# Keys and queries of an attention layer: turned by TensorE, or by VectorE in 32x32 blocks and a trip through memory

## The chip, the cores and the metric

The kernel runs on one core of a Trainium2 chip. The metric is the device time of one execution in microseconds (us). The core has five engines that each work through a queue of their own in order: TensorE (PE, matrix products), VectorE (DVE), ScalarE (ACT), GpSimd (POOL) and SyncE (SP, which here only issues transfers). An engine stops at an instruction whose semaphore has not been reached, and everything behind it on that engine stops too. Transfers are issued from SP and from ACT.

## What is computed

Two transformer layers on 1024 tokens of width 512: a linear attention (L0), a mixture of low-rank experts, a softmax attention (L1) and a gated MLP, each added to its input and normalised. The change lies in the third, L1, with 32 heads of 128:

```
q = rmsnorm((x @ Wq + bq).reshape(1024, 32, 128), gq)      # per head, over its 128 values
k = rmsnorm((x @ Wk + bk).reshape(1024, 32, 128), gk)
v = (x @ Wv + bv).reshape(1024, 32, 128)
p = softmax(q @ k.T / sqrt(128))                           # per head, 1024 x 1024
y = (p @ v) per head @ Wo + bo                             # summed over heads
```

Each product is made in three passes, high times high, high times low and low times high: an operand is split into a rounded part (`_hi`) and what is left (`_lo`).

## The kernel before

The tokens are eight tiles (t = 0 to 7) of 128; two tiles make a batch (i = 0 to 3). The program of L1 is written out by hand for each engine as one `step` per head, which has eight slots (s = 0 to 7); a loop (`Fori`) runs two steps per turn, and the steps at both ends are written out. In step h, the slots score head h against its keys, tile by tile, while the values and outputs of head h and of head h-1 before it follow some slots later, and while the next heads are projected. An even slot and the odd slot behind it are called a pair here; a step has four pairs.

What PE does in a slot, in this order: half a batch of values (in an even slot; in an odd slot this comes last), one tile of projection (`project_tile`: 12 matmuls of 384 columns into `b_pj_kq`), one tile of scores (6 matmuls of 512 columns into `b_s_ps`), in odd slots four transposes (`transpose_kq`, below), one tile of output (3 matmuls of 512 columns into `b_y_ps`).

The way of a batch of keys and queries, before: DVE takes the projected tile out of `b_pj_kq` with its bias into `b_nat` (`take`); ACT squares it (`square`), DVE sums (`means`), POOL takes the inverse root (`inverse_rms`), ACT scales (`scale_kq`); PE turns keys and queries of both tiles, 128x128 each, into the other half of `b_pj_kq` (`transpose_kq`, line 1718); ACT copies that to `b_k_hi` and, times a gain, to `b_q_hi` (`kq_high`), DVE subtracts for `b_k_lo` and `b_q_lo` (`kq_low`). The scores of the next head wait for the last batch of this.

The way of a probability tile, before and after: DVE takes the row maximum (`maxima`) from `b_s_ps`, ACT the exponential (`exponent`), DVE turns the tile in 32x32 blocks (`transpose_blocks`, one STREAM_TRANSPOSE), ACT issues a write of the blocks to a scratch tensor in memory (`write_blocks`, 512 KB), SP reads them back in four transfers of 128 KB that put the blocks into their place (`move`), ACT rounds (`prob_hi`), POOL subtracts (`prob_lo`), PE multiplies with the values. SP works through these moves in order; each waits for its write.

Two PSUM limits tie DVE to PE: there is one bank for projections, so `project_tile` waits until the tile before has been taken; and two for scores, so the scores of tile t wait for the exponential of tile t-2.

Of the kernel before, what the change touches and what calls it, by code (L numbers as in the profile page):

```python
# [36 lines left out]
P = 128  # L37
# [1307 lines left out]
def l1_attention(nc, sh, ln_in, ln, aw, mlp, w, ow, bias, bo, gains):  # L1345
# [16 lines left out]
    with ExitStack() as ctx:  # L1362
# [6 lines left out]
        def sem(name):  # L1369
# [16 lines left out]
        nat = [sb(f"nat{i}", [P, BATCH, KQV]) for i in range(NB)]  # L1386
# [26 lines left out]
        pj_kq = bank("pj_kq", [P, TOK])  # L1413
        pj, kq_ps = pj_kq[:, 0:HALF], pj_kq[:, HALF:].rearrange("p (k n) -> p k n", k=2)
# [22 lines left out]
        const_in, bias_added, gain_ready = sem("const_in"), sem("bias_added"), sem("gain_ready")  # L1437
# [5 lines left out]
        def y_bank(h, t):  # L1443

            return pj if peeled(h, HEADS - 1) and t >= 3 and t % 2 else y_ps[:, :]
# [52 lines left out]
        def v_batch(h, b, cur, nxt, s):  # L1498

            if s % 2 == 0:  # L1500
                return None
            if s < 5:
                return (h, b, NB - 2 + s // 2) if cur else None
            return (h + 1, 1 - b, (s - 5) // 2) if nxt else None

        SPLITS = {1: 0, 2: 1, 4: 2}
# [5 lines left out]
        def by_tile(tile):  # L1512

            return tile[:, :].rearrange("p (u g q) -> p g u q", g=GROUPS, u=BATCH)

# [3 lines left out]
        def _(sp):  # L1519
# [42 lines left out]
        def _(pool):  # L1562
            def inverse_rms(g, bg, i):

                pool.wait_ge(mean_ready, NB * g + i + 1)
                wait(pool, exp_done, NT * (g - 1))
# [4 lines left out]
            def v_low(g, bg, i):  # L1571
                pool.wait_ge(v_hi_done, NB * g + i + 1)
                wait(pool, pv, NB * (g - 1))
                pool.tensor_tensor(v_lo[bg][:, BATCH * i:BATCH * (i + 1), :], nat[i][:, :, 2 * HD:],
                                   f(v_hi[bg][:, BATCH * i:BATCH * (i + 1), :]), ALU.subtract).then_inc(v_lo_done, 1)

# [7 lines left out]
            def step(h, b, cur, rest, nxt, more):  # L1584
                for s in range(NT):
                    if nxt and s % 2 == 0:
                        inverse_rms(h + 1, 1 - b, s // 2)
                    if v_batch(h, b, cur, nxt, s):
                        v_low(*v_batch(h, b, cur, nxt, s))
                    if split_batch(h, cur, rest, s):  # L1590
                        for part in range(2):
                            prob_lo(*split_batch(h, cur, rest, s), part)
# [13 lines left out]
        def _(act):  # L1606
# [3 lines left out]
            def square(g, i):  # L1610
                act.wait_ge(taken, NT * g + BATCH * (i + 1))
                wait(act, summed, NB * g + i)
                act.activation(sq[:, :, :, :].rearrange("p t k d -> p t (k d)"), nat[i][:, :, 0:2 * HD],  # L1613
                               ACT.Square).then_inc(squared, 1)

            def kq_high(g, bg, i):
                cut = slice(i * WIDE, (i + 1) * WIDE)
                act.wait_ge(kq_tr, NB * g + i + 1)
                wait(act, scored, NT * (g - 1))
                act.activation(k_hi[bg][:, cut], kq_ps[:, 0, :], ACT.Copy)  # L1620
                act.activation(q_hi[bg][:, cut], kq_ps[:, 1, :], ACT.Copy, scale=gain[:, 0:1]).then_inc(kq_hi_done, 1)  # L1621

            def v_high(g, bg, i):
                act.wait_ge(taken, NT * g + BATCH * (i + 1))
                wait(act, pv, NB * (g - 1))
                act.activation(v_hi[bg][:, BATCH * i:BATCH * (i + 1), :], nat[i][:, :, 2 * HD:],
# [7 lines left out]
            def scale_kq(g, bg, i):  # L1634

                act.wait_ge(rstd_ready, NB * g + i + 1)
                for u in range(BATCH):
                    for k in range(2):
                        part = nat[i][:, u, k * HD:(k + 1) * HD]
# [23 lines left out]
            def step(h, b, cur, rest, nxt, more):  # L1663
                if peeled(h, -1):
                    act.wait_ge(gain_ready, 1)
                for s in range(NT):
                    if nxt and s % 2 == 0:
                        square(h + 1, s // 2)
                    if v_batch(h, b, cur, nxt, s):
                        v_high(*v_batch(h, b, cur, nxt, s))  # L1670
# [6 lines left out]
                    if nxt and s % 2 == 0:  # L1677
                        scale_kq(h + 1, 1 - b, s // 2)
# [6 lines left out]
                    if cur:  # L1685
                        exponent(h, b, s)
                    if cur and s == 3:
# [9 lines left out]
        def _(pe):  # L1697
# [49 lines left out]
            def output_tile(h, b, t):  # L1747
# [4 lines left out]
                wait(pe, y_added, NT * h + (t - 1 if peeled(h, HEADS - 1) and t >= 3 else t))  # L1752
# [3 lines left out]
            def step(h, b, cur, rest, nxt, more):  # L1756
                for s in range(NT):
# [6 lines left out]
                    if nxt and s % 2:  # L1764
# [457 lines left out]
```

## Time and profile before

| | |
|---|---|
| median of 3 runs | 3012.76 us (3007.79 to 3013.55) |
| the profiled execution, its own time | 3011.74 us |
| its span, first to last instruction | 3009.8 us |
| its mean granted TensorE clock | 0.990 |
| PE busy over the span | 96% |
| DVE, ACT, POOL busy over the span | 74%, 53%, 65% |
| L1 attention, roughly | 1150 to 2745 us of the span |

Busy time is an average over stages that have different limits, so the stage that the change touches is read by itself in the rows below. In the view of stretches, the columns after each engine's name are its busy us and, in brackets, its instructions; the last three are the granted clock, the mean busy share of the 16 DMA engines and the GB/s that they moved. In a timeline a row is the start, the duration, the engine, the line, the instruction and its tiles; what stands in brackets at the end is the engine's idle time before it and what ended it. Matmuls overlap, so PE's pace is read from the difference between two starts, not from a duration.

### The profile page before, as it was taken

The numbers are of one execution on the slowest core, as the hardware profiler recorded it, in microseconds if no ns is written. First come the engines' busy times: TensorE is split into PE (matmuls) and PEld (weight loads), VectorE is DVE, ScalarE is ACT, GpSimd is POOL, SyncE is SP. The second block draws the span as 40 slices with busy tenths as digits, with TensorE's granted clock in tenths as the row PEclk, the third lists the DMA queues.
The fourth block names the chain that finished last, engine by engine and source line by source line (L and its number), as shares of the span: only waits on it lengthen the run. The fifth ranks groups of instructions, "written<-read, shape, count | busy, mean of one in ns | idle before, by whom it ended". The sixth has DMA issues, their size and how long they took to land. (4 is left out here: it accounts for less than half of the span.)

```text
span 3009.8 us, 55475 instructions
## 1 busy us (share of the span) xinstructions
PE 2886.3 (96%) x15712; PEld 2506.9 (83%) x15712; DVE 2236.4 (74%) x3420; ACT 1590.8 (53%) x3145; POOL 1952.6 (65%) x1525
## 2 busy tenths in 40 slices
PE   7999999999999977999999999999999999986998
PEld 5888888888888857898899899989898989975886
DVE  6787887887887856777777777777777777775555
ACT  4444444444444423666666666666666666652221
POOL 7777777777777632666666666666656666655664
PEclk9999999999999999999999999999999999998999
DMA  4334334334334401665666656666666656555551
GB/s 123 116 107 122 101 106 122 101 106 122 101 106 122 123 25 51 198 209 193 204 203 200 204 194 202 196 204 204 196 203 197 204 191 207 194 193 181 151 144 41
DMA packets 310073, 464.10 MB, mean 154 GB/s; under 512 B 30464, under 2 KB 220928, under 8 KB 305792
## 3 DMA queue, kind: packets, MB, share of 16 engines
q1 hardware_dynamic: 272336, 328.37, 37.8%
q10 hardware_dynamic: 37680, 135.02, 11.3%
q8 instruction: 29, 0.48, 0.1%
q14 instruction: 28, 0.23, 0.0%
HBM read 293.41 MB, written 169.87 MB: 154 GB/s over the span
## 5 line engine op out<-in xcount | busy, mean ns | idle before, releaser
L1660 ACT ACTIVATE b_prob<-b_s_ps,b_shift 128x1024 f32<-128x1024 f32 x256 | 286.1, 1118 | 347.2 <-DVE b_shift L1810 339.5
L82 PE MATMUL b_pj_kq<-b_w_hi,xT_hi 128*128 128x384 f32 x1008 | 351.8, 349 | 26.4 <-DVE b_nat L1786 24.5
L83 PE MATMUL b_pj_kq<-b_w_lo,xT_hi 128*128 128x384 f32 x1008 | 343.0, 340 | 0.0
L84 PE MATMUL b_pj_kq<-b_w_hi,xT_lo 128*128 128x384 f32 x1008 | 342.7, 340 | 0.0
L1816 DVE STREAM_TRANSPOSE b_blocks<-b_prob 128x1024 f32<-128x1024 f32 x256 | 317.3, 1239 | 28.4 <-ACT b_prob L1660 27.8
L1567 POOL TENSOR_TENSOR b_rstd<-b_mean_sq,power 128x4 f32<-128x4 f32 x128 | 129.0, 1008 | 320.7 <-DVE b_mean_sq L1796 314.1
L1582 POOL TENSOR_TENSOR b_pT_lo<-b_pT_lo,b_pT_hi 128x1024 fp32r<-128x1024 f32 x128 | 305.0, 2405 | 19.4 <-ACT b_pT_hi L1649 19.4
L1582 POOL TENSOR_TENSOR pT_lo<-pT_lo,pT_hi 128x1024 fp32r<-128x1024 f32 x128 | 305.0, 2406 | 13.9 <-ACT pT_hi L1649 13.9
L1810 DVE TENSOR_REDUCE b_shift<-b_s_ps 128x1 f32<-128x1024 f32 x256 | 306.8, 1199 | 2.7 <-PE b_s_ps L84 2.7
L82 PEld LDWEIGHTS b_pj_kq<-b_w_hi,xT_hi 128*128 128x128 f32 x1008 | 190.4, 189 | 63.4 <-DVE b_nat L1786 48.1
L1341 POOL TENSOR_TENSOR b_w_lo<-b_w_raw,b_w_hi 128x512 fp32r<-128x512 f32 x96 | 124.1, 1294 | 152.0 <-ACT b_w_hi L1334 134.5
L1793 DVE TENSOR_REDUCE b_sq_sum<-b_sq 128x4 f32<-128x512 f32 x128 | 87.8, 686 | 174.2 <-ACT b_sq L1613 174.2
L82 PE MATMUL b_s_ps<-b_k_hi,b_q_hi 128*128 128x512 f32 x512 | 201.0, 393 | 7.4 <-ACT b_prob L1660 7.4
L502 POOL TENSOR_TENSOR e_lo<-e_store,e_lo 128x256 fp32r<-128x256 f32 (+1 forms) x96 | 102.6, 1082 | 160.5 <-ACT e_lo L597 160.5
L84 PE MATMUL b_s_ps<-b_k_hi,b_q_lo 128*128 128x512 f32 x512 | 202.4, 395 | 0.0
L83 PE MATMUL b_s_ps<-b_k_lo,b_q_hi 128*128 128x512 f32 x512 | 201.5, 394 | 0.0
L83 PEld LDWEIGHTS b_pj_kq<-b_w_lo,xT_hi 128*128 128x128 f32 x1008 | 190.8, 189 | 0.6
L84 PEld LDWEIGHTS b_pj_kq<-b_w_hi,xT_lo 128*128 128x128 f32 x1008 | 190.6, 189 | 0.0
L990 DVE TENSOR_TENSOR a_acc<-a_acc,a_y_ps 128x512 f32<-128x512 f32 x243 | 164.8, 678 | 31.0 <-PE a_y_ps L84 31.0
L1837 DVE SCALAR_TENSOR_TENSOR x_nat<-b_y_ps,b_row_inv,x_nat 128x512 f32<-128x512 f32 x253 | 186.1, 736 | 2.3 <-PE b_y_ps L84 2.1
L1802 DVE TENSOR_TENSOR b_k_lo<-b_pj_kq,b_k_hi 128x256 fp32r<-128x256 f32 x128 | 54.3, 424 | 158.5 <-ACT b_q_hi L1621 158.4
L1640 ACT ACTIVATE b_nat<-b_nat,b_rstd 128x128 f32<-128x128 f32 x512 | 163.1, 391 | 13.1 <-POOL b_rstd L1567 13.1
(345 smaller groups left out, 9382.6 us busy)
## 6 DMA issues: line engine op xcount, KB each, us to landing
bounce<-b_blocks ACTq DMA_DIRECT2D x256, 512.0 KB, 3.5
pT_lo<-bounce SPq DMA_DIRECT2D x512, 128.0 KB, 3.1
b_pT_lo<-bounce SPq DMA_DIRECT2D x512, 128.0 KB, 2.8
kv_bounce<-a_kv_blocks SPq DMA_DIRECT2D x128, 256.0 KB, 3.8
a_kv_raw<-kv_bounce SPq DMA_DIRECT2D x32, 1024.0 KB, 4.8
b_w_raw<-in_w SPq DMA_DIRECT2D x32, 768.0 KB, 5.1
b_w_raw<-in_w SPq DMA_DIRECT2D x95, 256.0 KB, 3.2
a_w_raw<-in_w SPq DMA_DIRECT2D x32, 256.0 KB, 3.1
```

The costliest lines, as they stand in the source:

```text
L82: pe.matmul(out, w_hi, x_hi, start=first, stop=False, skip_group_check=partial)
L83: pe.matmul(out, w_hi, x_lo, start=False, stop=False, skip_group_check=partial)
L84: return pe.matmul(out, w_lo, x_hi, start=False, stop=last, skip_group_check=partial)
L990: dve.tensor_tensor(acc[:, t, :], acc[:, t, :], y_bank(h, t)[:, :], ALU.add).then_inc(y_added, 1)
L1341: pool.tensor_tensor(self.lo[b][:, :, cut], self.raw[:, :, cut], f(self.hi[b][:, :, cut]), ALU.subtract).then_inc(self.lo_done, 1)
L1567: pool.tensor_tensor(rstd[bg][:, BATCH * i:BATCH * (i + 1), :].rearrange("p t k -> p (t k)"), mean_sq[:, :, :].rearrange("p t k -> p (t k) ...
L1582: pool.tensor_tensor(lo, f(lo), f(hi), ALU.subtract).then_inc(pT_lo_done, 1)
L1640: last = act.activation(part, part, ACT.Copy, scale=rstd[bg][:, BATCH * i + u, k:k + 1])
L1660: act.activation(prob[t % 2][:, :], s_ps[t % 2][:, :], ACT.Exp, bias=shift[:, t:t + 1], accum_out=row_sum[:, t:t + 1]).then_inc(exp_done, 1)
L1810: dve.tensor_reduce(shift[:, t:t + 1], s_ps[t % 2][:, :], AX_X, ALU.max, negate=True).then_inc(shift_done, 1)
L1816: dve.transpose(blocks[t % 2][:, :, :, :].rearrange("p a m q -> p m a q"), prob[t % 2][:, :].rearrange("p (m a q) -> p m a q", a=GROUPS, q ...
L1837: dve.scalar_tensor_tensor(out=sh.x_nat[:, t, :], in0=y_bank(h, t), scalar=row_inv[:, t:t + 1], in1=sh.x_nat[:, t, :], op0=ALU.mult, op1=A ...
```

## The change

The transposes on PE go. A batch of keys and queries now takes the way of the probabilities:

- DVE turns the scaled keys and queries of a batch in 32x32 blocks (`turn_kq`, two STREAM_TRANSPOSE of 128x256), in the even slot of the pair after the one that scaled them;
- ACT issues a write of 256 KB to a scratch tensor (`write_kq`), SP reads it back in four transfers of 64 KB, in runs of 512 bytes (`move_kq`), into `b_kq_raw`;
- ACT multiplies the queries there by the gain, in place, and copies keys and queries to their high parts (`kq_high`: three instructions instead of two);
- POOL makes the low parts (`kq_low`: two subtractions of 128x256), which DVE made before.

Projections run two slots earlier, the weights of a head are split one or two slots earlier, and `square`, `means`, `inverse_rms` and `scale_kq` run a pair earlier. The half PSUM tile that held the turned keys and queries becomes a second bank for the outputs. In DVE's slot the probability blocks come first and `means` and `take` after; on ACT `scale_kq` moves behind the exponential; on POOL `inverse_rms` moves between the two halves of `prob_lo`. SP's step begins at tile 4 of the head before.

```diff
+        def projected(h, b, nxt, more, s):
-            if s < 6:
-                return (h + 1, 1 - b, s + 2) if nxt else None
-            return (h + 2, b, s - 6) if more else None
+            if s < 4:
+                return (h + 1, 1 - b, s + 4) if nxt else None
+            return (h + 2, b, s - 4) if more else None
+        def prepared(h, b, nxt, more, s):
+            i = s // 2 + 1
+            if i < NB:
+                return (h + 1, 1 - b, i) if nxt else None
+            return (h + 2, b, 0) if more else None
+        def turned(h, b, nxt, s):
+            return (h + 1, 1 - b, s // 2) if nxt and s % 2 == 0 else None
-        SPLITS = {1: 0, 2: 1, 4: 2}
+        SPLITS = {0: 0, 1: 1, 2: 2}
...
+            def move_kq(g, i):
+                sp.wait_ge(kq_written, 16 * (NB * g + i + 1))
+                sp.sem_inc(room, 1)
+                wait(sp, kq_lo_done, NB * g + i - 1)
+                for c in range(GROUPS):
+                    sp.dma_start(kq_raw[i % 2][c * BLK:(c + 1) * BLK].rearrange("y r k u x -> y r (k u x)"),
+                                 kq_bounce[i % 2][:, :, c, :].rearrange("r y n -> y r n")).then_inc(kq_moved, 16)
...
+                for t in range(NT // 2, NT):
+                    if t == 5 and cur:
+                        move_kq(h, 3)
+                    if t == 7 and nxt:
+                        move_kq(h + 1, 0)
+                    if rest:
+                        move(h - 1, t)
+                for t in range(NT // 2):
+                    if t % 2 and nxt:
+                        move_kq(h + 1, t // 2 + 1)
                     if cur:
                         move(h, t)
...
+            def kq_low(g, bg, i):
+                cut = slice(i * WIDE, (i + 1) * WIDE)
+                pool.wait_ge(kq_hi_done, 2 * (NB * g + i + 1))
+                pool.tensor_tensor(in_blocks(k_lo[bg][:, cut]), from_blocks(i, 0), f(in_blocks(k_hi[bg][:, cut])),
+                                   ALU.subtract)
+                pool.tensor_tensor(in_blocks(q_lo[bg][:, cut]), from_blocks(i, 1), f(in_blocks(q_hi[bg][:, cut])),
+                                   ALU.subtract).then_inc(kq_lo_done, 1)
...
             def kq_high(g, bg, i):
                 cut = slice(i * WIDE, (i + 1) * WIDE)
-                act.wait_ge(kq_tr, NB * g + i + 1)
+                act.wait_ge(kq_moved, 16 * GROUPS * (NB * g + i + 1))
                 wait(act, scored, NT * (g - 1))
-                act.activation(k_hi[bg][:, cut], kq_ps[:, 0, :], ACT.Copy)
-                act.activation(q_hi[bg][:, cut], kq_ps[:, 1, :], ACT.Copy, scale=gain[:, 0:1]).then_inc(kq_hi_done, 1)
+                scaled = kq_raw[i % 2][:, :, 1, :, :].rearrange("p r u x -> p r (u x)")
+                act.activation(scaled, scaled, ACT.Copy, scale=gain[:, 0:1]).then_inc(kq_hi_done, 1)
+                act.activation(in_blocks(k_hi[bg][:, cut]), from_blocks(i, 0), ACT.Copy)
+                act.wait_ge(kq_hi_done, 2 * (NB * g + i) + 1)
+                act.activation(in_blocks(q_hi[bg][:, cut]), from_blocks(i, 1), ACT.Copy).then_inc(kq_hi_done, 1)
+            def write_kq(g, i):
+                act.wait_ge(kq_blocked, 2 * (NB * g + i + 1))
+                wait(act, kq_written, 16 * (NB * g + i))
+                wait(act, kq_moved, 16 * GROUPS * (NB * g + i - 1))
+                act.dma_start(kq_bounce[i % 2][:, :, :, :].rearrange("r y c n -> (r y) (c n)"),
+                              kq_blocks[i % 2][:, :, :, :, :].rearrange("p c k u x -> p (c k u x)")).then_inc(
+                    kq_written, 16)
...
-            def transpose_kq(g, i):
-                pe.wait_ge(kq_scaled, NB * g + i + 1)
-                wait(pe, kq_lo_done, NB * g + i)
-                for kind in range(2):
-                    for u in range(BATCH):
-                        last = pe.transpose(kq_ps[:, kind, u * P:(u + 1) * P], nat[i][:, u, kind * HD:(kind + 1) * HD],
-                                            sh.ident[:, :])
-                last.then_inc(kq_tr, 1)
...
-                wait(pe, y_added, NT * h + (t - 1 if peeled(h, HEADS - 1) and t >= 3 else t))
+                wait(pe, y_added, NT * h + t - 1)
...
-            def kq_low(g, bg, i):
-                cut = slice(i * WIDE, (i + 1) * WIDE)
-                dve.wait_ge(kq_hi_done, NB * g + i + 1)
-                dve.tensor_tensor(k_lo[bg][:, cut], kq_ps[:, 0, :], f(k_hi[bg][:, cut]), ALU.subtract)
-                dve.scalar_tensor_tensor(out=q_lo[bg][:, cut], in0=kq_ps[:, 1, :], scalar=gain[:, 0:1],
-                                         in1=f(q_hi[bg][:, cut]), op0=ALU.mult,
-                                         op1=ALU.subtract).then_inc(kq_lo_done, 1)
+            def turn_kq(g, bg, i):
+                dve.wait_ge(kq_scaled, NB * g + i + 1)
+                wait(dve, kq_written, 16 * (NB * g + i - 1))
+                for k in range(2):
+                    dve.transpose(kq_blocks[i % 2][:, :, k, :, :].rearrange("p c u x -> p u c x"),
+                                  nat_of(bg, i)[:, :, k * HD:(k + 1) * HD].rearrange(
+                                      "p u (c y) -> p u c y", c=GROUPS)).then_inc(kq_blocked, 1)
```

How the rows stand on the engines. On DVE, inside the loop, an odd slot and the even slot behind it read like this before (`b_shift` is the row maximum, `x_nat` the sum of the outputs, `b_sq_sum` the sum of squares, `b_nat` the taken projection):

```order
L1816 STREAM_TRANSPOSE b_blocks<-b_prob 128x8x4x32
L1802 TENSOR_TENSOR b_k_lo<-b_pj_kq,b_k_hi 128x256
L1803 SCALAR_TENSOR_TENSOR b_q_lo<-b_pj_kq,b_gain,b_q_hi 128x256
...
L1810 TENSOR_REDUCE b_shift<-b_s_ps 128x1
...
L1837 SCALAR_TENSOR_TENSOR x_nat<-b_y_ps,b_row_inv,x_nat 128x512
...
L1793 TENSOR_REDUCE b_sq_sum<-b_sq 128x4
...
L1796 TENSOR_SCALAR b_mean_sq<-b_sq_sum 128x4
...
L1786 TENSOR_TENSOR b_nat<-b_pj_kq,b_bias 128x384
L1828 TENSOR_TENSOR b_o_lo<-b_o_ps,b_o_hi 128x4x2x32
L1816 STREAM_TRANSPOSE b_blocks<-b_prob 128x8x4x32
```

And now:

```order
L1876 STREAM_TRANSPOSE b_blocks<-b_prob 128x8x4x32
...
L1884 RECIPROCAL b_row_inv<-b_row_sum 128x2
...
L1845 TENSOR_TENSOR b_nat<-b_pj_y,b_bias 128x384
...
L1870 TENSOR_REDUCE b_shift<-b_s_ps 128x1
...
L1897 SCALAR_TENSOR_TENSOR x_nat<-b_y_ps,b_row_inv,x_nat 128x512
...
L1863 STREAM_TRANSPOSE b_kq_blocks<-b_nat 128x2x4x32 x2
L1876 STREAM_TRANSPOSE b_blocks<-b_prob 128x8x4x32
L1888 TENSOR_TENSOR b_o_lo<-b_o_ps,b_o_hi 128x4x2x32
...
L1852 TENSOR_REDUCE b_sq_sum<-b_sq 128x4
...
L1855 TENSOR_SCALAR b_mean_sq<-b_sq_sum 128x4
...
L1845 TENSOR_TENSOR b_nat<-b_pj_y,b_bias 128x384
```

Nothing of the keys stands any more between the probability blocks and the maximum of an odd slot; the even slot begins with the two block turns and the probability blocks, and the take comes last of these.

On ACT, the odd slot before (`b_prob` is the exponential):

```order
L1626 ACTIVATE b_v_hi<-b_nat 128x256
L1654 DMA bounce<-b_blocks 128x1024
L1620 ACTIVATE b_k_hi<-b_pj_kq 128x256
L1621 ACTIVATE b_q_hi<-b_pj_kq,b_gain 128x256
...
L1660 ACTIVATE b_prob,b_row_sum<-b_s_ps,b_shift 128x1024
```

and now, with the first row of the even slot behind it (a split of weights stands between them here):

```order
L1720 DMA bounce<-b_blocks 128x1024
...
L1675 ACTIVATE b_kq_raw<-b_kq_raw,b_gain 128x4x64
L1676 ACTIVATE b_k_hi<-b_kq_raw 128x256
...
L1678 ACTIVATE b_q_hi<-b_kq_raw 128x256
...
L1726 ACTIVATE b_prob,b_row_sum<-b_s_ps,b_shift 128x1024
L1334 ACTIVATE b_w_hi<-b_w_raw 128x4x128
...
L1685 DMA kq_bounce<-b_kq_blocks 128x512
```

The exponential of an odd slot stands behind the high parts of the keys as before, and these now wait for a transfer instead of for PE; the write of the next batch stands behind that exponential.

## Rows read from the trace of the kernel before

**Rows 1.** Stretches: 100 us inside the loop of L1.

```profile
1900.00:2000.00 100.00, 98.54 (x580) 89.74 (x579) 75.69 (x117) 64.59 (x132) 65.17 (x42) 1.00 0.61 198
```

**Rows 2.** Timeline of PE: one pair, from one set of transposes to the next.

```profile
1902.07 0.60 PE L1718 MATMUL b_pj_kq<-ident,b_nat 128*128 128x128 f32 x4
1902.42 0.48 PE L82 MATMUL b_y_ps<-b_ow_hi,b_o_hi 128*128 128x512 f32 x1
...
1903.21 0.28 PE L82 MATMUL b_o_ps<-b_pT_hi,b_v_hi 128*128 128x256 f32 x1
...
1906.12 0.34 PE L82 MATMUL b_pj_kq<-b_w_hi,xT_hi 128*128 128x384 f32 x1
...
1908.24 0.39 PE L82 MATMUL b_s_ps<-b_k_hi,b_q_hi 128*128 128x512 f32 x1
...
1909.63 0.40 PE L82 MATMUL b_y_ps<-b_ow_hi,b_o_hi 128*128 128x512 f32 x1
...
1910.33 0.34 PE L82 MATMUL b_pj_kq<-b_w_hi,xT_hi 128*128 128x384 f32 x1
...
1913.84 0.60 PE L1718 MATMUL b_pj_kq<-ident,b_nat 128*128 128x128 f32 x4
```

**Rows 3.** Timeline of ACT: an instruction that comes once per head, 28 heads apart.

```profile
1258.54 0.62 ACT L1690 ACTIVATE b_ow_hi<-b_ow_raw 128x512 fp32r<-128x512 f32 x1
...
2606.14 0.62 ACT L1690 ACTIVATE b_ow_hi<-b_ow_raw 128x512 fp32r<-128x512 f32 x1
```

**Rows 4.** Waits, 1300 to 2600 us: total us, times, longest us.

```profile
PEld b_pj_kq L82 <- DVE b_nat L1786: 46.8, 86, 1.3
PE b_pj_kq L82 <- DVE b_nat L1786: 15.9, 52, 0.9
ACT b_pT_hi L1649 <- DMA b_pT_lo<-bounce: 13.8, 20, 2.1
```

**Rows 5.** Timeline of DVE: an odd slot's end and the even slot behind it.

```profile
1904.86 0.42 DVE L1802 TENSOR_TENSOR b_k_lo<-b_pj_kq,b_k_hi 128x256 fp32r<-128x256 f32 x1 [1.25 <-ACT b_q_hi L1621]
...
1905.59 1.21 DVE L1810 TENSOR_REDUCE b_shift<-b_s_ps 128x1 f32<-128x1024 f32 x1
1906.72 0.74 DVE L1837 SCALAR_TENSOR_TENSOR x_nat<-b_y_ps,b_row_inv,x_nat 128x512 f32<-128x512 f32 x1
1908.60 0.69 DVE L1793 TENSOR_REDUCE b_sq_sum<-b_sq 128x4 f32<-128x512 f32 x1 [1.13 <-ACT b_sq L1613]
...
1910.32 1.24 DVE L1816 STREAM_TRANSPOSE b_blocks<-b_prob 128x1024 f32<-128x1024 f32 x1
```

**Rows 6.** DMA, 1300 to 2600 us: packets, MB, share; issues, KB each, us to landing.

```profile
q1 hardware_dynamic: 136080, 146.93, 39.9%
q10 hardware_dynamic: 31104, 113.26, 22.0%
...
bounce<-b_blocks ACTq DMA_DIRECT2D x216, 512.0 KB, 3.6
...
b_pT_lo<-bounce SPq DMA_DIRECT2D x432, 128.0 KB, 2.8
```

**Rows 7.** Timeline of SP: the four issues of one tile's move.

```profile
1907.57 1.73 SPq L1537 DMA_DIRECT2D b_pT_lo<-bounce  x4
```

**Rows 8.** Timeline of ACT: an exponential, and the two halves of a rounding.

```profile
1906.84 1.12 ACT L1660 ACTIVATE b_prob<-b_s_ps,b_shift 128x1024 f32<-128x1024 f32 x1 [2.01 <-DVE b_shift L1810]
...
1908.73 2.00 ACT L1649 ACTIVATE pT_hi<-pT_lo 128x1024 fp32r<-128x1024 f32 x2
```

**Rows 9.** One line on POOL: min, median, max of one in ns.

```profile
L1574 POOL TENSOR_TENSOR b_v_lo<-b_nat,b_v_hi x128: 726/747/784, 1179.5 to 2693.3; 128x256 fp32r<-128x256 f32 x128
```

**Rows 10.** Timelines of ACT and DVE: the start of L1.

```profile
1164.94 1.28 ACT L1640 ACTIVATE b_nat<-b_nat,b_rstd 128x128 f32<-128x128 f32 x4 [2.11 <-POOL b_rstd L1567]
...
1191.18 1.23 DVE L1810 TENSOR_REDUCE b_shift<-b_s_ps 128x1 f32<-128x1024 f32 x1 [0.83 <-PE b_s_ps L84]
...
1202.93 1.18 DVE L1810 TENSOR_REDUCE b_shift<-b_s_ps 128x1 f32<-128x1024 f32 x1
```

More of the change, by code:

```diff
@@ L1496, in output, with v_batches @@
             return (h - 1, 1 - b, s + 1) if rest else None
[L1498 to L1504, printed above, removed]
-        SPLITS = {1: 0, 2: 1, 4: 2}
+        def v_batches(h, b, cur, nxt, s):
+            if s == 1:
+                return ((h, b, 3),) if cur else ()
+            which = {5: (0, 1), 7: (2,)}.get(s, ())
+            return [(h + 1, 1 - b, i) for i in which] if nxt else ()
+        SPLITS = {0: 0, 1: 1, 2: 2}
         def by_group(tile):
@@ L1585, in step @@
                 for s in range(NT):
[L1586 to L1589, printed above, removed]
+                    for which in v_batches(h, b, cur, nxt, s):
+                        v_low(*which)
+                    if nxt and s % 2:
+                        kq_low(h + 1, 1 - b, s // 2)
                     if split_batch(h, cur, rest, s):
-                        for part in range(2):
-                            prob_lo(*split_batch(h, cur, rest, s), part)
+                        prob_lo(*split_batch(h, cur, rest, s), 0)
+                    if s % 2 == 0 and prepared(h, b, nxt, more, s):
+                        inverse_rms(*prepared(h, b, nxt, more, s))
+                    if split_batch(h, cur, rest, s):
+                        prob_lo(*split_batch(h, cur, rest, s), 1)
                     if cur and s == 3:
@@ L1664, in step @@
                 if peeled(h, -1):
-                    act.wait_ge(gain_ready, 1)
+                    act.wait_ge(gain_and_bias, 1)
                 for s in range(NT):
[L1667 to L1670, printed above, removed]
+                    ready = prepared(h, b, nxt, more, s)
+                    if turned(h, b, nxt, s):
+                        write_kq(h + 1, s // 2)
+                    if s % 2 == 0 and ready:
+                        square(*ready)
+                    for which in v_batches(h, b, cur, nxt, s):
+                        v_high(*which)
                     q = quarter(h, b, cur, rest, s)
@@ L1686, in step @@
                         exponent(h, b, s)
+                    if s % 2 == 0 and ready:
+                        scale_kq(*ready)
                     if cur and s == 3:
@@ L1844, in step @@
                     dve.tensor_scalar(gain[:, :], gain[:, :], float(HD) ** -0.5, None,
-                                      ALU.mult).then_inc(gain_ready, 1)
-                    dve.wait_ge(gain_ready, 1)
+                                      ALU.mult).then_inc(gain_and_bias, 1)
+                    dve.wait_ge(gain_and_bias, 1)
                 for s in range(NT):
                     q = quarter(h, b, cur, rest, s)
-                    if nxt and s % 2 == 0:
-                        means(h + 1, s // 2)
+                    ready = prepared(h, b, nxt, more, s)
+                    if turned(h, b, nxt, s):
+                        turn_kq(*turned(h, b, nxt, s))
+                    if rest and s == 0:
+                        transpose_blocks(h - 1, NT - 1)
+                    if cur and s:
+                        transpose_blocks(h, s - 1)
+                    if q and not q[3]:
+                        invert_sums(q[0], q[2])
+                    if q and q[3]:
+                        out_lo(q[0], q[2])
+                    if s % 2 == 0 and ready:
+                        means(ready[0], ready[2])
                     if projected(h, b, nxt, more, s):
```

76 lines of the change are left out of this document (35 added, 41 removed).

## Prediction, made before the changed kernel ran

> **What bounds the kernel now.** First the view of stretches, inside the loop of L1: over 100 us PE is busy 98.5 us, DVE 75.7, ACT 64.6, POOL 65.2, the DMA engines 0.61, at full granted clock [rows 1]. PE is the bound, and the others have a quarter of their time free or more. Then PE's timeline over one pair, to see of what its time is made. It runs without a gap from 1902.07 to 1913.84, so a pair without waits takes 11.77 us [rows 2]. By the starts, four transposes take 0.35 us, an output 0.70 (1909.63 to 1910.33) but 0.79 behind transposes, two halves of values 2.91, a projection 2.12, scores 1.39 [rows 2]. Third, the pace: 28 heads lie between 1258.54 and 2606.14 [rows 3], which is 48.13 us a head and 12.03 a pair. So 12.03 - 11.77 = 0.26 us of each pair is waiting. The view of waits says for what: PE's projections wait for DVE to take the tile before, 15.9 us by the matmuls and 46.8 by the weight loads that run ahead of them, over 27 heads [rows 4]; 0.26 x 4 x 27 = 28 us lies between the two. Fourth, DVE: why is it late, with a quarter of its time free? In an odd slot it stands still 1.25 us until ACT has made the high parts of keys and queries, then makes the low ones, and only then comes to the maximum; in the even slot it waits 1.13 us for squares [rows 5].
>
> **Part 1, the transposes.** Sixteen per head go, four per pair: 0.35 us and the 0.09 by which the output behind them is slower. PE's pair becomes 11.77 - 0.44 = 11.33 us.
>
> **Part 2, PE's remaining waits.** Let 0 be the start of an even slot's projection. Then PE ends that at 2.12, scores at 3.51, the output at 4.21, the odd projection at 6.33, scores at 7.72, the output at 8.42, values at 11.33. DVE after the change: the even maximum (1.13 us by the starts in [rows 5]) from 3.7, to which I add 0.1 to 0.2 us of my own for each hand-over here and below, exponential of 1.12 [rows 8] to 6.1, blocks of 1.24 [rows 5] to 7.35, row inverse and take to 8.1, odd maximum to 9.25, sum of outputs to 9.9, turns of 0.7 (below) to 10.6, blocks to 11.8. What follows, low outputs, means and take, took 1.72 us in all before [rows 5]; the first two end at about 13.2, which is 1.9 of the next pair, when the projection (2.12) is not yet done. The take ends at about 2.7 and PE needs the bank at 4.21. That leaves 1.5 us, so I take the wait as gone: 0.26 us more. Bounds: 0 (it stays) and 0.26. I take the upper end because both things that made DVE late leave its queue at this point. Per pair 0.44 + 0.26 = 0.70 us; over the 112 pairs of [rows 3] 78.7 us, and 49 at the lower bound.
>
> **Part 3, the load of each engine per pair, against 11.33.** DVE loses the low parts, 0.73 us (1904.86 to 1905.59), and gets two turns of 128x256: a quarter of the 1.24 us of a 128x1024 turn, 0.31, or as long as the 128x256 subtraction, 0.42 [rows 5]. I take 0.35 each, and DVE stays at 0.757 x 12.03 = 9.1. ACT has 0.646 x 12.03 = 7.8, plus a third copy of 128x256 (two 128x1024 ones take 2.00 [rows 8], so 0.25 at least; I take 0.4) and an issue: 8.6. POOL has 7.8, plus two subtractions of 128x256 at 0.75 [rows 9]: 9.3. They read runs of 32 values, which row 9 doesn't; at twice the price POOL has 10.8, which still fits. SP's issues: two moves at 1.73 [rows 7] and a third of as many transfers: 5.2.
>
> **Part 4, the DMA engines.** They are busy 0.399 + 0.220 of the time [rows 6], 7.45 us per pair. A write of 512 KB costs 0.22 x 1300 / 216 = 1.32 us of all sixteen, so one of 256 KB 0.7 to 0.9. On the other queue, 864 moves of 128 KB are 113 of 147 MB; if the other 34 MB cost what written ones cost (2.5 us a MB, 85 us), a move costs (519 - 85) / 864 = 0.50 us. One of 64 KB has as many rows, half as long: 0.25 if the bytes count, 0.50 if the rows do, so 1.0 to 2.0 for four. The sum is 9.2 to 10.4 of 11.33; I take 9.8. They stay below PE, at 0.86.
>
> The Trainium skill speaks against this: "DMA: Bandwidth & Descriptors", section Bandwidth, tells to batch transfers and calls those under 64 KB descriptor-dominated, with 0.95 us of busy time for one of 64 KB. By that figure, four would take 3.8 us and the DMA engines 12.0 per pair, and they would bound the kernel at today's pace. Here 128 KB moves cost 0.50 [rows 6], half of that for twice the bytes, so I go by the row.
>
> **Part 5, the new wait.** The high parts wait on ACT for a trip through memory. Queued behind them is the odd exponential; DVE's blocks and, two tiles on, PE's scores wait for it. The trip: a write 3.6 us (median of 512 KB [rows 6]), SP's fourth issue 1.3 after the first (three quarters of 1.73 [rows 7]), landing 2.8 [rows 6]: 7.7 us. The write stands behind the odd exponential, at 10.6, and the keys land at 18.3, which is 7.0 of the next pair. ACT comes to the high parts at about 7.4, behind the write of the even tile's blocks; three copies, 1.1 us by my estimate from part 3, end at 8.5, and the odd maximum is there at 9.25. So the trip is hidden by DVE's work, with 0.75 us to spare, and by 1.5 more before PE waits. As a loop: trip 7.7, copies 1.1, exponential 1.1, hand-overs 0.3, 10.2 of 11.33. The probabilities' loop is rounding 2.0, write 3.6, 1.3, 2.8, 0.3: 10.0; before, scaling (1.28 [rows 10]) stood in it too, and ACT did wait for it 20 times in 27 heads [rows 4]. The last batch's low parts end on POOL at 10 to 10.8, and the next head's scores start at 13.45. Price: 0 by this; if the cover goes, each us of trip beyond 8.8 costs one per pair.
>
> The second output bank is worth nothing: the waits show none of PE for the sum of outputs.
>
> **Part 6, the ends.** At the start nothing covers the trips. The first batch is scaled at 1166.2 [rows 10]; each write stands on ACT behind the copies of the batch before, so four trips follow one another. With 7.1 us each (transfers alone in the queues, my choice between 6.7 and 7.7), copies 1.1: 32.8, plus turns 0.7, low parts 1.5, scores 1.4: the first maximum at 1202.6 instead of 1191.18 [rows 10], 11.4 later. Head 0's first three pairs took 11.75 (1191.18 to 1202.93 [rows 10]), without values or outputs; now the loop of 10.2 holds them: 4.7 back. At the end two more pairs gain 0.7 each; the rest I leave as it is.
>
> **Sum.** -78.7 + 11.4 - 4.7 - 1.4 = -73.4. The profiled execution took 3011.7 us (the median is 1.0 more), which makes 2938.
>
> **Rivals.** (a) Only the transposes' time comes: a short wait stays on PE, since DVE's slack of 1.5 us hangs on an exponential behind a transfer. For it speaks that both loops fill 90% of the pair; against it, that they ran at 94% before. -49 + 5 = -44: 2968. (b) The DMA engines become the bound, by the page's rule: the four reads cost 3.8 us instead of 1 to 2. Pair 7.45 + 0.8 + 3.8 = 12.05, and with the start 3017, no change or just above. Against it: each row would have to cost twice what one of double length costs [rows 6]. (c) Slower: the trip, at 0.86 busy DMA engines, takes longer than 9.5 us. From there trip + 2.5 is over 12.03; at 10.5 a pair takes 13.0, +0.97 x 112 + 7 = +116: 3127. For it: write, read and the blocks' transfers share queues, and SP serves them in order, so one late write delays the next move. Against it: the trip may grow by 1.8 us before it decides.
>
> **Chances.** The forecast 0.64, (a) 0.20, (b) 0.06, (c) 0.10. The forecast's own range is 2918 to 2958: from no cost at the start and a little gain at the end, to 20 us of small waits. Up to 2985 it takes in (a) as well, which makes 8 in 10 for 2918 to 2985. A measurement here tells about 0.2%, 6 us, from no change: faster 0.86 (forecast, (a), a little of (b)), same 0.03, slower 0.11.
>
> **What would show it.** Part 1: PE's timeline without transposes, 11.33 us between two even projections. Part 2: no waits of PE for `b_nat`, 45.3 us between the rows that come once per head. Part 3: turns of 0.31 to 0.42 on DVE, low parts of 0.75 on POOL. Part 4: DMA share about 0.86. Part 5: no idle of ACT before the scaled copy with a DMA as releaser; if that row leads the waits, (c) or (a) holds. Part 6: the first maximum near 1202. I am wrong if 64 KB reads take far longer to land than 2.8 us, or if runs of 32 values slow POOL more than twofold.

## The result, and the profile after

The changed kernel takes 3020.27 us (median of 7 runs, 3016.47 to 3026.70), the kernel before beside it 3013.55 (7 runs): a ratio of 1.0029, 95% interval 1.0018 to 1.0040. It is 0.3% slower. The forecast was 2938, with 0.11 for slower.

First the view of stretches after, the 100 us of [rows 1]:

```profile
1900.00:2000.00 100.00, 95.73 (x558) 87.01 (x557) 89.97 (x118) 69.29 (x142) 76.13 (x60) 1.00 0.82 248
```

PE still waits, 4.3 us of 100, and DVE went from 75.7 to 90.0, where the prediction had it unchanged. ACT, POOL and DMA are where it had them. The pace, by ACT's row that comes once per head:

```profile
1262.69 0.62 ACT L1759 ACTIVATE b_ow_hi<-b_ow_raw 128x512 fp32r<-128x512 f32 x1
...
2616.04 0.62 ACT L1759 ACTIVATE b_ow_hi<-b_ow_raw 128x512 fp32r<-128x512 f32 x1
```

These are 28 heads, 48.33 us each and 12.08 a pair, against 12.03 in [rows 3]. The waits of 1300 to 2600 us (total, times, longest) say what PE waits for:

```profile
PEld b_pj_y L82 <- DVE b_nat L1845: 103.9, 98, 1.3
PE b_pj_y L82 <- DVE b_nat L1845: 61.4, 98, 0.8
ACT b_kq_raw L1675 <- DMA b_kq_raw<-kq_bounce: 15.6, 29, 1.2
```

The wait for the take, which the prediction took as gone, has more than doubled by the weight loads and nearly quadrupled by the matmuls [rows 4]. ACT hardly waits for the new transfers. So why is DVE late? Its timeline in an even slot, and beside it POOL's:

```profile
1904.12 0.42 DVE L1888 TENSOR_TENSOR b_o_lo<-b_o_ps,b_o_hi 128x256 fp32r<-128x256 f32 x1 [0.45 <-ACT b_o_hi L1698]
1904.46 0.68 DVE L1852 TENSOR_REDUCE b_sq_sum<-b_sq 128x4 f32<-128x512 f32 x1
1905.17 2.36 DVE L1855 TENSOR_SCALAR b_mean_sq<-b_sq_sum 128x4 f32<-128x4 f32 x1
1907.44 0.55 DVE L1845 TENSOR_TENSOR b_nat<-b_pj_y,b_bias 128x384 f32<-128x384 f32 x1
1907.91 1.21 DVE L1870 TENSOR_REDUCE b_shift<-b_s_ps 128x1 f32<-128x1024 f32 x1
```

```profile
1905.11 2.39 POOL L1633 TENSOR_TENSOR b_pT_lo<-b_pT_lo,b_pT_hi 128x1024 fp32r<-128x1024 f32 x1 [2.42 <-ACT b_pT_hi L1715]
1907.68 1.01 POOL L1609 TENSOR_TENSOR b_rstd<-b_mean_sq,power 128x4 f32<-128x4 f32 x1 [0.18 <-DVE b_mean_sq L1855]
1908.66 2.40 POOL L1633 TENSOR_TENSOR b_pT_lo<-b_pT_lo,b_pT_hi 128x1024 fp32r<-128x1024 f32 x1
```

The mean of squares, four values per partition, takes 2.36 us. It starts 0.06 us after POOL's first low half and ends at 1907.53, 0.03 after that half (1905.11 + 2.39 = 1907.50). The take behind it ends 4.97 us after the start of the projection (1903.02); PE wants the bank at 4.21, and it waits:

```profile
1903.02 0.34 PE L82 MATMUL b_pj_y<-b_w_hi,xT_hi 128*128 128x384 f32 x1
...
1906.51 0.40 PE L82 MATMUL b_pj_y<-b_ow_hi,b_o_hi 128*128 128x512 f32 x1
...
1908.04 0.44 PE L82 MATMUL b_pj_y<-b_w_hi,xT_hi 128*128 128x384 f32 x1 [0.67 <-DVE b_nat L1845]
...
1915.20 0.35 PE L82 MATMUL b_pj_y<-b_w_hi,xT_hi 128*128 128x384 f32 x1
```

From the output to the odd projection lie 1.53 us instead of 0.70: 0.83 late, and the pair of 12.18 us (1903.02 to 1915.20) is 11.33 and this, to 0.02. It is so over the whole loop. One line's view of the mean (min, median, max in ns) after, and then before:

```profile
L1855 DVE TENSOR_SCALAR b_mean_sq<-b_sq_sum x128: 169/2366/2403, 1162.6 to 2666.8; 128x4 f32<-128x4 f32 x128
```

```profile
L1796 DVE TENSOR_SCALAR b_mean_sq<-b_sq_sum x128: 169/171/214, 1163.7 to 2666.4; 128x4 f32<-128x4 f32 x128
```

In the changed kernel 113 of the 128 means take longer than 0.25 us, and each of them ends 0.02 to 0.03 us after a subtraction on POOL: 109 after a low half, four after one of weights or of queries. POOL's timeline before, a row that the prediction did not read:

```profile
1909.56 1.01 POOL L1567 TENSOR_TENSOR b_rstd<-b_mean_sq,power 128x4 f32<-128x4 f32 x1 [5.32 <-DVE b_mean_sq L1796]
1910.54 4.77 POOL L1582 TENSOR_TENSOR pT_lo<-pT_lo,pT_hi 128x1024 fp32r<-128x1024 f32 x2
```

Before, the root stood ahead of both low halves, so POOL stands idle here for 5.32 us until the mean is done, and no mean of that run overlaps a low half: 66 of the 128 run with POOL idle, and 62 meet the last 0.2 us of a subtraction of weights and take at most 0.21 us. The change put the root between the halves, and the first half now runs beside the mean.

### The profile page after: what moved, and what is told of

Same layout as the page of the kernel before. It is cut to its first block and busy times, and to the rows that moved or that the text cites. A ratio compares the mean times of both kernels' runs of the same rounds, so it can differ in the third digit from the quotient of the medians.

```text
span 3014.5 us, 56400 instructions
## 1 busy us (share of the span) xinstructions
PE 2835.3 (94%) x15200; PEld 2448.4 (81%) x15200; DVE 2455.1 (81%) x3420; ACT 1646.1 (55%) x3273; POOL 2142.2 (71%) x1781
## 5 line engine op out<-in xcount | busy, mean ns | idle before, releaser
L82 PE MATMUL b_pj_y<-b_w_hi,xT_hi 128*128 128x384 f32 x1008 | 355.2, 352 | 83.2 <-DVE b_nat L1845 74.8
L83 PE MATMUL b_pj_y<-b_w_lo,xT_hi 128*128 128x384 f32 x1008 | 342.8, 340 | 0.0
L84 PE MATMUL b_pj_y<-b_w_hi,xT_lo 128*128 128x384 f32 x1008 | 341.9, 339 | 0.0
L82 PEld LDWEIGHTS b_pj_y<-b_w_hi,xT_hi 128*128 128x128 f32 x1008 | 190.5, 189 | 134.4 <-DVE b_nat L1845 107.0
L1855 DVE TENSOR_SCALAR b_mean_sq<-b_sq_sum 128x4 f32<-128x4 f32 x128 | 262.7, 2052 | 4.4
L83 PEld LDWEIGHTS b_pj_y<-b_w_lo,xT_hi 128*128 128x128 f32 x1008 | 191.0, 189 | 0.4
L84 PEld LDWEIGHTS b_pj_y<-b_w_hi,xT_lo 128*128 128x128 f32 x1008 | 190.4, 189 | 0.0
L82 PE MATMUL b_o_ps<-pT_hi,b_v_hi 128*128 128x256 f32 x512 | 146.2, 285 | 5.9 <-POOL pT_lo L1633 5.9
L82 PE MATMUL b_o_ps<-b_pT_hi,b_v_hi 128*128 128x256 f32 x512 | 145.3, 284 | 6.4 <-POOL b_pT_lo L1633 6.4
```

The costliest lines, as they stand in the source:

```text
L82: pe.matmul(out, w_hi, x_hi, start=first, stop=False, skip_group_check=partial)
L83: pe.matmul(out, w_hi, x_lo, start=False, stop=False, skip_group_check=partial)
L84: return pe.matmul(out, w_lo, x_hi, start=False, stop=last, skip_group_check=partial)
L1855: dve.tensor_scalar(mean_sq[:, :, :], sq_sum[:, :, :], 1.0 / HD, L1_EPS, ALU.mult, ALU.add).then_inc(means_done, 1)
```

## The experiments

Three theories. **1**: the mean is held by POOL's low half, since both use memory that only one of them may use at a time; the take behind it is late. **2**: the trip through memory is too long, and what waits for it makes DVE late (rival (c)). **3**: an instruction at this place in DVE's new order is slow by its semaphores or its turn, whatever POOL does.

| kernel | median, us | ratio to before, 95% interval | us per head |
|---|---|---|---|
| changed | 3020.27 | 1.0029 (1.0018 to 1.0040) | 48.33 |
| e1 root ahead of both halves | 2929.84 | 0.9724 (0.9710 to 0.9737) | 45.31 |
| e2 sums in PSUM | 2932.13 | 0.9735 (0.9720 to 0.9750) | 45.32 |
| e3 changed, no trip | 3010.94 | 0.9996 (0.9987 to 1.0005) | 48.37 |
| e4 before, POOL busy beside the mean | 3178.96 (one run) | | 53.33 |
| e5 e1, no trip | 2920.89 | 0.9694 (0.9681 to 0.9708) | 45.42 |
| e6 changed, take ahead of means | 2980.65 | 0.9898 (0.9881 to 0.9916) | 46.98 |
| e7 e1, blocks late | 2983.72 | 0.9906 (0.9891 to 0.9921) | 46.83 |
| e8 e1, one output at a time | 2930.93 | 0.9729 (0.9716 to 0.9742) | 45.26 |
| e9 e6, no trip | 2944.44 | 0.9785 (0.9771 to 0.9798) | 45.87 |
| e10 e7, no trip | 2946.38 | 0.9787 (0.9774 to 0.9800) | 45.79 |

The last column is the difference of ACT's once-per-head row over 28 heads. e1 to e4 ran together, then e5 to e8, then e9 and e10; before took 3011.57, 3012.36 and 3012.03 beside them.

**e1**, GpSimd's order alone:

```diff
                     if split_batch(h, cur, rest, s):
-                        prob_lo(*split_batch(h, cur, rest, s), 0)
                     if s % 2 == 0 and prepared(h, b, nxt, more, s):
                         inverse_rms(*prepared(h, b, nxt, more, s))
                     if split_batch(h, cur, rest, s):
-                        prob_lo(*split_batch(h, cur, rest, s), 1)
+                        for part in range(2):
+                            prob_lo(*split_batch(h, cur, rest, s), part)
```

> The changed kernel with one thing moved: on GpSimd the inverse root stands ahead of both halves of the probabilities' subtraction again, as before the change, instead of between them. Theory 1 (port): the small mean on VectorE, 2.37 us by the median instead of 0.17, waits for GpSimd's subtraction, which began just before it and holds the SBUF port that the mean wants; with the root first, GpSimd stands still until the mean is done, so the mean takes 0.17, VectorE takes the projection 2 us earlier, PE's wait of 0.83 a pair goes, a pair takes 11.33 to 11.5 us and the kernel 2930 to 2955. Theory 2 (trip): the mean's length is a symptom, the pair is held by the trip of the keys through memory and the queues that serve it; the pair stays at 12.0 or more, the kernel at 3005 to 3025.

The mean's line, the stretch and the waits of 1300 to 2500 us in e1:

```profile
L1854 DVE TENSOR_SCALAR b_mean_sq<-b_sq_sum x128: 170/170/943, 1162.7 to 2577.7; 128x4 f32<-128x4 f32 x128
```

```profile
1900.00:2000.00 100.00, 100.00 (x589) 93.19 (x588) 80.46 (x124) 73.33 (x153) 80.49 (x62) 1.00 0.90 265
```

```profile
POOL b_rstd L1609 <- DVE b_mean_sq L1854: 166.1, 107, 2.8
...
DVE b_nat L1844 <- PE b_pj_y L84: 30.9, 81, 0.5
...
ACT b_kq_raw L1674 <- DMA b_kq_raw<-kq_bounce: 54.5, 46, 3.9
...
PEld b_pj_y L82 <- DVE b_nat L1844: 2.2, 4, 0.6
```

90 us come back, although POOL again waits 166.1 us for the mean. PE is busy all the time, now the take waits for PE, and a pair takes 45.31 / 4 = 11.33 us, which is part 1's figure. A theory with the trip or DVE's new order as its cause fails here: neither was touched. Twelve means are still long, up to 0.94 us; each ends 0.02 to 0.03 us after a subtraction of weights or queries on POOL, so it is not the low half alone that holds them.

**e2** keeps the change's order on POOL, and puts the sums of squares into PSUM, in a free part of the bank of `b_o_ps` (PE waits for the mean before it writes there again):

```diff
-        sq_sum = sb("sq_sum", [P, BATCH, 2])
+        sq_sum = o_ps[:, WIDE:WIDE + 2 * BATCH].rearrange("p (t k) -> p t k", k=2)
...
```

> The changed kernel with the four sums of squares in PSUM instead of SBUF (spare columns of the values' bank, with a wait on PE so that nothing else is in that bank), GpSimd's order as changed. Theory 1 (port): an instruction with its source in PSUM doesn't want the port that GpSimd holds; the mean takes 0.2 us beside the running subtraction, the kernel 2930 to 2960. Theory 2 (trip): 3005 to 3025. A third (3): any instruction of VectorE at this place is slow, because of its semaphores or its turn: the mean stays near 2.3 us.

DVE, and POOL beside it:

```profile
1911.62 0.16 DVE L1858 TENSOR_SCALAR b_mean_sq<-b_o_ps 128x4 f32<-128x4 f32 x1
1911.82 0.56 DVE L1848 TENSOR_TENSOR b_nat<-b_pj_y,b_bias 128x384 f32<-128x384 f32 x1
```

```profile
1911.21 2.40 POOL L1633 TENSOR_TENSOR b_pT_lo<-b_pT_lo,b_pT_hi 128x1024 fp32r<-128x1024 f32 x1 [1.41 <-ACT b_pT_hi L1715]
1913.58 1.00 POOL L1609 TENSOR_TENSOR b_rstd<-b_mean_sq,power 128x4 f32<-128x4 f32 x1
```

The mean runs in the middle of POOL's half and takes 0.16 us; so do all 128, 102 of which overlap a low half. So the overlap by itself, or POOL's order, is not enough, and theory 3 falls here too: the same operation on four values is held when its source lies in SBUF, and is not when it lies in PSUM.

**e3** leaves out the write and the reads (their issues go too, not shown); the high and low parts take DVE's tile, so keys and queries are turned only within blocks, which isn't the reference's computation.

```diff
-            return kq_raw[i % 2][:, :, kind, :, :].rearrange("p r u x -> p u r x")
+            return kq_blocks[i % 2][:, :, kind, :, :].rearrange("p r u x -> p u r x")
...
-                act.wait_ge(kq_moved, 16 * GROUPS * (NB * g + i + 1))
+                act.wait_ge(kq_blocked, 2 * (NB * g + i + 1))
```

> The changed kernel without the trip: ScalarE and GpSimd read the blocks where VectorE left them, nothing is written to memory and read back, so keys and queries are not turned across blocks. GpSimd's order as changed. Theory 1 (port): the mean stays at 2.0 to 2.4 us and the pair at 11.9 to 12.1; only the start is shorter, by 5 to 12 us: 3000 to 3015. Theory 2 (trip): the pair falls to 11.3 to 11.5: 2920 to 2945.

```profile
L1847 DVE TENSOR_SCALAR b_mean_sq<-b_sq_sum x128: 170/2365/2378, 1161.8 to 2657.9; 128x4 f32<-128x4 f32 x128
```

Without any trip a head takes 48.37 us, and the mean is as long as in the changed kernel. Of the 9.3 us that come, 8.85 come ahead of head 1's row (1253.84 instead of 1262.69). Theory 2 falls.

**e4** does the reverse: the kernel before, with a subtraction of 128x1024 on POOL, ahead of the root, from the time on when the squares are there. It adds work that the reference doesn't have.

```diff
+                pool.wait_ge(squared, NB * g + i + 1)
+                pool.tensor_tensor(held[:, :], f(sh.xT_hi[:, 0, :]), f(sh.xT_hi[:, 1, :]), ALU.subtract)
                 pool.wait_ge(mean_ready, NB * g + i + 1)
```

> The kernel before, with one more subtraction of 128x1024 on GpSimd ahead of each inverse root, begun when the squares are there, its result unused. It ends some 1.6 us after VectorE comes to the mean. Theory 1 (port): the mean takes 1.4 to 2.0 us instead of 0.17 in this kernel too, which has no trip and no third copy. Theories 2 and 3: it stays at 0.17, since nothing on VectorE or in the DMA queues is changed. The time tells little, as the root itself is later under each: 3080 to 3250.

DVE, and POOL beside it:

```profile
1925.88 1.74 DVE L1799 TENSOR_SCALAR b_mean_sq<-b_sq_sum 128x4 f32<-128x4 f32 x1
```

```profile
1925.20 2.40 POOL L1567 TENSOR_TENSOR b_held<-xT_hi 128x1024 f32<-128x1024 f32 x1 [2.17 <-ACT b_sq L1616]
1927.70 1.01 POOL L1570 TENSOR_TENSOR b_rstd<-b_mean_sq,power 128x4 f32<-128x4 f32 x1
```

The mean ends at 1927.62, POOL's work on quite other data at 1927.60. Over the run:

```profile
L1799 DVE TENSOR_SCALAR b_mean_sq<-b_sq_sum x128: 170/1606/2003, 1163.1 to 2831.8; 128x4 f32<-128x4 f32 x128
```

Two cases lie in this line. In 66 of the 128 the added subtraction starts 0.39 to 0.88 us ahead of the mean, and the mean takes 1.53 to 2.00 us. In the other 62 the mean starts first, by 0.08 to 0.15 us, and takes 0.17 to 0.21. So the hold can be made without any of the change, and it falls on a mean that comes second. The time itself says less, since the root is also late by POOL's 2.4 us.

**e5** prices the trip where PE is the bound: e1 with e3's edit.

> The kernel of e1_root_first (inverse root ahead of both low halves) without the write to memory and the four reads: the high and low parts take the turned blocks straight from VectorE's tile, so keys and queries are not turned across blocks and the output is not the reference's. It prices the trip where TensorE is the bound. If the trip is hidden in the loop, as the prediction had it, the heads keep 45.3 us and only the start gains, 5 to 9 us: 2920 to 2926 against e1's 2930. If ScalarE's 54.5 us of waiting for the keys' transfers in e1 still cost something, the heads come below 45.2 us and the time below 2915.

8.95 us less than e1, the heads no faster (45.42, against 45.31); head 1's row is 9.84 earlier (1251.38 against 1261.22). In the loop the trip is free, as part 5 had it, although ACT waits for it 54.5 us.

**e6** asks by what the long mean costs time: the take is put ahead of it, POOL keeps the change's order.

```diff
-                    if s % 2 == 0 and ready:
-                        means(ready[0], ready[2])
                     if projected(h, b, nxt, more, s):
                         take(*projected(h, b, nxt, more, s))
+                    if s % 2 == 0 and ready:
+                        means(ready[0], ready[2])
```

> The changed kernel with one exchange in VectorE's slot: the take of the projection ahead of sum and mean of squares; GpSimd keeps the order of the change, so the mean still starts beside GpSimd's first low half and is still stretched (I expect a median of 1.0 to 1.3 us, since the take and the sum now come first and the half ends at the same time). If what costs is that the take is late, TensorE's waits for the projection go and the time falls to 2928 to 2945, 45.3 to 45.6 us a head. If what costs is that the inverse root, and so the scaling and the next trip, come late, or that VectorE is held at all, the time stays above 3000.

DVE, POOL beside it, and the waits of 1300 to 2500 us:

```profile
1905.19 0.67 DVE L1852 TENSOR_REDUCE b_sq_sum<-b_sq 128x4 f32<-128x512 f32 x1
1905.89 2.06 DVE L1855 TENSOR_SCALAR b_mean_sq<-b_sq_sum 128x4 f32<-128x4 f32 x1
1907.86 1.21 DVE L1870 TENSOR_REDUCE b_shift<-b_s_ps 128x1 f32<-128x1024 f32 x1
```

```profile
1905.52 2.40 POOL L1633 TENSOR_TENSOR pT_lo<-pT_lo,pT_hi 128x1024 fp32r<-128x1024 f32 x1 [1.91 <-ACT pT_hi L1715]
```

```profile
PEld b_s_ps L82 <- ACT b_prob L1726: 13.5, 15, 1.5
...
PEld b_o_ps L82 <- POOL b_pT_lo L1633: 9.1, 26, 0.4
PEld b_o_ps L82 <- POOL pT_lo L1633: 8.8, 21, 0.6
...
PE b_s_ps L82 <- POOL b_q_lo L1625: 8.8, 15, 1.2
...
PEld b_pj_y L82 <- DVE b_nat L1845: 6.1, 28, 0.3
```

A miss between the two sides. The wait for the take is nearly gone (6.1 us), as expected, but only 40 of e1's 90 us come. The mean is shorter by 0.5 us only (median 1897 ns, not 1.0 to 1.3): in the rows above it starts 0.37 us into POOL's half. And the maxima behind it come later than in the changed kernel, 3.7 us after the start of their scores by the median of 1300 to 2500 us, instead of 1.9. PE's wait is spread over exponentials, low halves and the next head's keys.

**e9** tells which of these: e6 with e3's edit.

> The kernel of e6_take_ahead_of_means without the trip through memory (keys and queries not turned across blocks, as in e3, so the output is not the reference's). In e6 the waits for the projection went and 47 us a head stayed; this tells which late thing holds it. If the late mean acts by the keys' trip (mean, root, scaling, turns, write, reads, keys' low parts, scores of the next head), the heads fall to 45.3 to 45.8 us and the time to 2920 to 2940. If VectorE's own hold does it (late maxima, late exponentials, late blocks and low halves), the heads stay at 46.5 to 47 and the time only loses the start, 2965 to 2975.

36.2 us less than e6, 5.7 of it ahead of head 1's row (1260.73 against 1266.42), and 45.87 us a head, just over what was expected. With the trip, a late mean behind the take costs 1.67 us a head (e6 against e1); without it, 0.44 (e9 against e5). So in the loop most of e6's rest goes by the trip. That it does so because the late mean makes root, scaling, turns, write and reads late, until they are hidden no more, is the likely way, not shown step by step. What is left of e9 above e5, 12 us over the 28 heads and 9.4 ahead of head 1's row, is not resolved.

**e7** is e1 with `transpose_blocks` moved behind `means` and `take` in DVE's slot, the part of the change that says "blocks first".

> The kernel of e1_root_first with the probability blocks back behind means and take in VectorE's slot. In e1 the even slot's take stands 0.3 to 0.4 us waiting for TensorE, and then 0.8 us are free ahead of the maximum; blocks of 1.25 us behind the take fill this and make the even maximum 0.3 to 0.5 us late, and the blocks themselves 3 us later. If the slack of about 1.5 us that the prediction worked out stands, TensorE feels nothing: 2928 to 2945, 45.3 to 45.6 us a head. If the order of the blocks carries the gain, TensorE waits for maxima or for the values: 46 us a head or more, 2950 and above.

```profile
ACT b_kq_raw L1674 <- DMA b_kq_raw<-kq_bounce: 105.7, 48, 7.7
...
PEld b_s_ps L82 <- ACT b_prob L1725: 27.0, 19, 5.2
PE b_s_ps L82 <- POOL b_q_lo L1625: 21.1, 19, 4.9
...
PEld b_pj_y L82 <- DVE b_nat L1844: 5.9, 22, 0.3
```

A miss: 54 us slower than e1, so the 1.5 us of slack in part 2 do not cover late blocks. It goes with ACT's waits for the keys' transfers, up to 7.7 us, twice those of e1 in sum; behind them stand the exponential and the keys for which PE waits up to 5 us.

**e10** is e7 with e3's edit.

> The kernel of e7_root_first_blocks_late without the trip (output not the reference's, as in e3). In e7 the keys' transfers kept ScalarE waiting 105.7 us instead of 54.5 and TensorE's few waits are long, up to 5.2 us, for the exponential and the keys. If late blocks cost by the moves of the keys that wait behind the blocks' moves in SyncE's queue, the time falls to e5's, 2918 to 2930, 45.3 to 45.6 us a head. If late blocks cost by themselves (maxima behind them, values late), the heads stay above 46.3 and the time at 2960 to 2975.

37.3 us less than e7, between the two sides; but 9 of these come by leaving the trip out of e1 too. With the trip late blocks cost 53.9 us (e7 against e1), without it 25.5 (e10 against e5), so about half of their cost hangs on the keys' trip; by the pace more, 1.52 and 0.36 us a head. In e10 ACT waits for the moves of the probabilities (48.5 and 33.1 us in 1300 to 2500 us; 7.1 and 0.3 in e1). That these make up the rest is not shown.

**e8** is e1 with each output waiting for the sum of the one before (`NT * h + t` for `NT * h + t - 1` in the wait ahead of `three_pass`).

> The kernel of e1_root_first in which each output waits for the sum of the output before it, as before the change, so that the second output bank brings nothing. The prediction priced the bank at nothing: 2925 to 2935, no difference from e1. If the bank does carry something now that a pair takes 11.33 us, TensorE shows waits for the sum of outputs and the heads come above 45.5 us, 2940 or more.

2930.93, no difference: the second bank brings nothing.

## Why the prediction was wrong

**The step that failed** is in part 2: "What follows, low outputs, means and take, took 1.72 us in all before". The sum took over the time of the mean, 0.17 us, as something that goes with the instruction; it took 2.37, because POOL's order changed beside it. On the prediction's own schedule, 2.2 us more put the end of the mean at 4.1 instead of 1.9 and the end of the take at some 4.6, 0.4 past the 4.21 at which PE needs the bank. In the changed kernel DVE also comes to the mean later than on that schedule, 2.13 us after the start of the projection (median of 1300 to 2500 us) instead of about 1.7; in the rows above it waits 0.45 us for the high outputs first. So the take ends at 4.97, and PE is 0.83 late. In e1, without the hold, DVE comes to the mean at 1.90, and PE hardly waits. Part 3's "DVE stays at 9.1" is wrong by the same term: 0.90 x 12.08 = 10.9. The order on POOL was known, but the row of before that tells what it had kept apart, POOL idle for 5.32 us until the mean, is not among the prediction's rows.

The Trainium skill has the rule, on "SBUF — State Buffer", section Who interferes with whom: VectorE's two-port modes, which `tensor_scalar` can enter, contend with GpSimd, and whichever issues first keeps the shared pair of ports for its whole instruction while the other blocks. The traces agree: the mean ends 0.03 us after POOL's half in the changed kernel and 0.02 after POOL's work in e4, and in e4 it is held only where that work began first. In the same section the Trainium skill names a reduction as free of this on this chip. The trace agrees here too: the sum of squares in e6 took 0.67 us, though it ended 0.34 us into POOL's half (1905.52, 2.40 long). Ports themselves, and the mode in which the mean ran, no run shows; what e1, e2 and e4 show is that for this mean the hold needs POOL's work at the same time and a source in SBUF.

**Part 1** was right: 11.33 us a pair in e1 and e2. **Part 2's gain of 0.26** was right where the mean is short: 2.2 us of the wait for the take are left in e1. **Part 3**, the other loads, in e1 by its stretch: DVE 0.805 x 11.33 = 9.1 as predicted, ACT 8.3 (8.6), POOL 9.1 (9.3); the two turns take 0.76 (0.70), a low part 0.73 to 0.76 (0.75). **Part 4**: the two queues in the changed kernel, 1300 to 2600 us,

```profile
q1 hardware_dynamic: 197993, 175.00, 52.6%
q10 hardware_dynamic: 46370, 140.79, 28.0%
...
b_kq_raw<-kq_bounce SPq DMA_DIRECT2D x432, 64.0 KB, 3.1
kq_bounce<-b_kq_blocks ACTq DMA_DIRECT2D x107, 256.0 KB, 2.1
```

are 0.806 x 12.08 = 9.7 us a pair (9.8); in e1 the share is 0.90 of 11.33, 10.2 us. A read of 64 KB adds (0.526 - 0.399) x 1300 / 432 = 0.38 us of all sixteen engines to the queue's time in [rows 6]. Its own packets, of 512 bytes, take 0.30; the rest is mostly that the other transfers of this queue got slower, those of 128 KB from 0.46 to 0.49. Both lie between the bounds of 0.25 and 0.50. Rival (b) is refuted by this, and by e1's pace. The 0.95 us that the Trainium skill gives for a transfer of 64 KB ("DMA: Bandwidth & Descriptors", section Bandwidth) were measured on transfers issued from GpSimd; for these reads, issued from SP, the measured 0.30 to 0.38 decides.

**Part 5**: the trip is hidden in the loop (e3, e5), but the "0.75 us to spare" holds only while DVE is on time. In the loop the trip costs nothing from e5 to e1, some 31 us from e9 to e6, some 29 from e10 to e7 (by the pace: 1.11 and 1.04 us a head, 28 heads). One term of the trip was too large: its write landed after 2.1 us (the row above), not the 3.6 of 512 KB. **Part 6**: the first maximum came at 1198.90, 7.7 late and not 11.4. The first trip took 5.4 us (write issued at 1166.50, copies at 1171.93) and not 7.1; the fourth write came 3.2 us late, since ACT waited for DVE's turns.

**The sum, measured.** In the changed kernel, by ACT's rows: +4.2 up to head 1, +5.8 over 28 heads, -5.2 behind them. In e1: +2.7, then 28 x (45.31 - 48.13) = -79.0, against -78.7 predicted, then -5.8; the span is 82 us shorter, not 73, because the start (+6.7 predicted) and the end (-1.4) were each some 4 us better. So the loop came out as forecast but for a term that the forecast didn't have, +3.02 us a head. Rivals (a) and (c) name other mechanisms, the wait behind a transfer and the trip; none of the rivals was what happened.

## What to carry to other kernels

When a change reorders two engines, ask of each small instruction what will now run beside it on the other engine, and not only how long it took where it stood; an idle stretch that costs nothing can be what kept two instructions apart. For a small operation that is held like this mean of four values, two ways out were measured: ahead of GpSimd's long work, with GpSimd waiting (e1), or with its source in PSUM (e2). And a transfer that is hidden is hidden by slack that other engines make: here it cost nothing in the loop or some 30 us, by whether VectorE's slot was on time.

## What was not expected of the hardware

A TENSOR_SCALAR of 0.17 us on 128x4 values took up to 2.40 us beside a GpSimd subtraction of 2.4 us, and 0.16 with its source in PSUM. Reading from SBUF is not enough for this. GpSimd was not slowed (a low half took 2.40 us by the mean in the changed kernel, 2.41 before), nor were, beside its subtractions, VectorE's sum of squares (0.67) and its block turn (1.25 at 1910.48 in the changed kernel, while GpSimd worked from 1908.66 to 1911.06), nor a RECIPROCAL of 128x2 values from SBUF to SBUF (0.12 to 0.16 us in e1, where 127 of 128 ran beside GpSimd's work). Four reads of 64 KB in runs of 512 bytes took 1.2 us of the sixteen DMA engines by their own packets, against 1.85 for four of 128 KB before: about two thirds of the time for half of the bytes.
